# A recommendation tower: Gram products on four strips of the TensorE array in place of two halves, and layer 2 of the last cycle in another order

## The reference

```python
e = jnp.stack([tbl_f[ids[:, f]] for f in range(27)], axis=1)       # (2048, 27, 128)
interactions = jnp.einsum('bnd,bmd->bnm', e, e)                    # a Gram matrix per sample
z = interactions[:, i, j]                                          # i, j: upper triangle, 351 products
h = jnp.concatenate([z, dense_ctx], axis=1)                        # 367 columns
h = jnp.maximum(h @ W_top1 + b_top1, 0.0)                          # 512
h = jnp.maximum(h @ W_top2 + b_top2, 0.0)                          # 256
y = h @ W_top3                                                     # (2048, 1)
```

## Time and profile before

| | |
|---|---|
| median of 3 runs | 348.53 us (348.14 to 349.94) |
| span of the profiled execution | 346.3 us |
| PE busy | 331.1 us, 96% of the span |
| POOL busy | 242.9 us, 70% |
| DVE busy | 219.4 us, 63% |
| ACT busy | 184.7 us, 53% |
| granted TensorE clock, mean | 1.000 |

### The profile page before, as it was taken

One profiled execution on the slowest core, in us unless ns is written; L12 is line 12 of the kernel. 1 busy time (PEld: TensorE's weight loads), 2 busy tenths in 40 slices (PEclk: granted clock), 3 DMA queues, 4 the chain that ended last, 5 costly groups with the idle time before them and its releaser, 6 DMA issues.

```text
span 346.3 us, 8212 instructions
## 1 busy us (share of the span) xinstructions
PE 331.1 (96%) x3478; PEld 282.8 (82%) x3478; DVE 219.4 (63%) x160; ACT 184.7 (53%) x315; POOL 242.9 (70%) x263
## 2 busy tenths in 40 slices
PE   2899999999999999999999999999999999998995
PEld 1667878887898888887898889887888889997894
DVE  5899997599427971499626991399724990360021
ACT  4898975533646354633646355633447346554521
POOL 6777777777777777777777777777777777777200
PEclk9999999999999999999999999999999999999999
DMA  6975795655237772768229772677327552572440
GB/s 169 222 178 168 225 252 142 156 157 135 67 55 157 146 158 55 107 173 178 83 55 157 146 160 55 89 197 177 83 57 134 131 112 57 85 168 72 85 81 8
DMA packets 53981, 44.06 MB, mean 127 GB/s; under 512 B 39810, under 2 KB 43983, under 8 KB 53945
## 3 DMA queue, kind: packets, MB, share of 16 engines
q1 hardware_dynamic: 43993, 26.52, 35.1%
q0 software_dynamic: 8192, 16.79, 21.3%
q10 hardware_dynamic: 1760, 0.22, 0.4%
HBM read 36.43 MB, written 7.09 MB: 126 GB/s over the span
## 4 chain that ended last, share of the span: by engine, by line
PE 86%; DMA 6%; SPq 3%; ACT 2%; issue 1%; DVE 1%; DVEq 0%
PE emb_ps L572 21%; PE emb_ps L574 20%; PE gram_ps L600 16%; PE mlp_ps L617 11%; PE mlp_ps L626 7%; PE emb_ps L583 7%; DMA h<-tbl_rows 3%; DMA products<-gram 1%; DMA gram<-tbl_rows 1%; PE emb_ps L644 1%; SPq L376 1%; DMA z<-products 1%; SPq L369 1%; PE mlp_ps L671 1%; PE mlp_ps L655 1%
## 5 line engine op out<-in xcount | busy, mean ns | idle before, releaser
L543 POOL DMA_INDIRECT rows<-tbl_rows,idx x256 | 242.0, 945 | 78.9 <-issue 74.4
L747 DVE TENSOR_TENSOR onehot<-ids_b,row_id 125x2048 fp32r<-125x2048 int32 x72 | 158.9, 2279 | 33.3 <-PE emb_ps L574 33.3
L572 PE MATMUL emb_ps<-onehot,table_hi 125*128 125x512 f32 (+1 forms) x400 | 147.6, 378 | 5.6 <-DVE table_lo L768 4.0
L574 PE MATMUL emb_ps<-onehot,table_lo 125*128 125x512 f32 (+1 forms) x400 | 143.0, 367 | 0.0
L572 PEld LDWEIGHTS emb_ps<-onehot,table_hi 125*128 125x128 f32 x400 | 76.0, 190 | 21.5 <-DVE table_lo L768 4.8
L574 PEld LDWEIGHTS emb_ps<-onehot,table_lo 125*128 125x128 f32 x400 | 76.1, 190 | 10.7
L600 PEld LDWEIGHTS gram_ps<-emb 128*54 128x54 f32 x2048 | 53.6, 130 | 5.6 <-issue 3.5
L600 PE MATMUL gram_ps<-emb 128*54 128x54 f32 x2048 | 55.8, 214 | 1.7 <-ACT emb L852 0.8
L851 ACT COPY held<-emb_ps 128x256 f32<-128x256 f32 x38 | 14.1, 371 | 75.9 <-PE emb_ps L574 75.8
L784 DVE TENSOR_TENSOR mlp_ps<-mlp_ps,rows 128x256 f32<-128x256 f32 x14 | 6.1, 433 | 76.5 <-PE mlp_ps L626 76.5
L882 ACT COPY gram<-gram_ps 118x432 f32<-118x432 f32 x64 | 33.2, 519 | 39.5 <-PE gram_ps L600 39.2
(11 more groups left out here) (49 smaller groups left out, 102.6 us busy)
## 6 DMA issues: line engine op xcount, KB each, us to landing
ids_b<-ids_onehot SPq DMA_DIRECT2D x33, 256.0 KB, 5.5
products<-gram SPq DMA_DIRECT2D x28, 216.0 KB
gram<-tbl_rows SPq DMA_DIRECT2D x9, 480.0 KB
rows<-tbl_rows,idx POOLq DMA_INDIRECT x256, 2.9
z<-products SPq DMA_DIRECT2D x14, 126.0 KB
h<-tbl_rows SPq DMA_DIRECT2D x2, 480.0 KB
z<-products SPq DMA_DIRECT2D x7, 112.0 KB
w_sb<-w SPq DMA_DIRECT2D x1, 768.0 KB, 5.8
```

Source lines behind the costliest of these rows:

```text
L543: pool.indirect_dma_start(out=rows[:, t, f, :], out_offset=None, in_=gathered_tables[f], in_offset=bass.IndirectOffsetOnAxis(ap=idx[:, p, ...
L572: nc.tensor.matmul(ps[:, 0:width], table_hi[0:ROWS, k, j, :], columns[:, c, :], start=j == 0, stop=False)
L574: last = nc.tensor.matmul(ps[:, 0:width], table_lo[0:ROWS, k, j, :], columns[:, c, :], start=False, stop=j == ROWS_PER - 1)
L747: nc.vector.tensor_tensor(onehot[0:ROWS, seq % ONEHOT_RING, 0:own * width].rearrange("p (j b) -> p j b", b=width), *operands, ALU.is_equal ...
```

## The change

`gram_products` takes one sample at a time. Its 27 columns go to one of four strips of 32 columns of the array and so to PSUM rows 0, 32, 64 or 96 onward. A tile has 128 products in two banks in place of 64 in four, and no mixed blocks. ACT copies a bank in one instruction of 123x432 elements. `gram` takes half the space and shares a tile with the staging buffers of the tables. What is stored and loaded per transfer stays the same size.

In the last cycle, the first tile's part of layer 2 of pair 6 moves from behind the Gram products to both sides of the last turn: two of its four products ahead of it, two behind. ACT's two copies of the dense features move ahead of the copies of the last Gram banks. The third load of the last tile's `z` is issued by ACT instead of SP, and the last tile's layer 1 takes its three steps in the order 0, 2, 1.

```diff
-HALVES, ABREAST = 2, 2
-QUARTERS = HALVES * ABREAST
+STRIPS, STRIP_ROWS = 4, 32
+QUARTERS = STRIPS
 GROUPS = P // QUARTERS
-GRAM_COLS = ABREAST * NF
-HALF_ROWS = P // HALVES
-GRAM_PART = HALF_ROWS + GRAM_COLS
-GROUPS_A_BANK = 8
+GRAM_PART = (STRIPS - 1) * STRIP_ROWS + NF
+GROUPS_A_BANK = 16
...
+LAST_STEPS = ((0, 1, 2), (0, 2, 1))
...
+        def load_step(engine, t, step):
+            first, end = step_places(step)
+            engine.dma_start(z[first:end, step, t * P:(t + 1) * P], tile_entries(t, step)
+                             ).then_inc(last_z_loaded[t][step], 16)
...
-                for step in range(STEPS):
-                    first, end = step_places(step)
-                    sp.dma_start(z[first:end, step, c0:c0 + P], tile_entries(t, step)
-                                 ).then_inc(last_z_loaded[t][step], 16)
+                for step in range(STEPS if t == 0 else STEPS - 1):
+                    load_step(sp, t, step)
...
-                        for half in range(HALVES):
-                            first = group * QUARTERS + half * ABREAST
-                            samples = emb[:, t, first:first + ABREAST, :].rearrange("d s f -> d (s f)")
-                            last = nc.tensor.matmul(
-                                ps[half * HALF_ROWS:half * HALF_ROWS + GRAM_COLS, b * GRAM_COLS:(b + 1) * GRAM_COLS],
-                                samples, samples, start=True, stop=True)
+                        for strip in range(STRIPS):
+                            sample = emb[:, t, group * QUARTERS + strip, :]
+                            row = strip * STRIP_ROWS
+                            last = nc.tensor.matmul(ps[row:row + NF, b * NF:(b + 1) * NF], sample, sample,
+                                                    start=True, stop=True)
...
+            def layer2_part(p, t, k0, k1):
+
+                pe.wait_ge(mlp_taken, p * M1 + M1)
+                for k in range(k0, k1):
+                    last = nc.tensor.matmul(mlp_ps[t][:, 0:HID2], h1[:, k, t * P:(t + 1) * P], w2_sb[:, k, :],
+                                            start=k == 0, stop=k == M1 - 1)
+                if k1 == M1:
+                    last.then_inc(mlp_full, 1)
...
                         layer1(p - 1, m)
-                        turn(p, 1, m)
+                        if p == LAST and m == M1 - 1:
+                            layer2_part(p - 1, 0, 0, M1 // 2)
+                            turn(p, 1, m)
+                            layer2_part(p - 1, 0, M1 // 2, M1)
+                        else:
+                            turn(p, 1, m)
...
-            layer2(LAST - 1)
+            layer2_part(LAST - 1, 1, 0, M1)
...
                 if p < LAST:
                     take_gram(p, 0)
                     place_dense(p)
+                else:
+                    place_dense(LAST)
                 take_gram(p, 1)
...
-            place_dense(LAST)
             for t in range(TILES):
                 for m in range(M1):
                     take_last_layer1(t, m)
+                if t == 0:
+
+                    act.wait_ge(last_products_out[TILES - 1], QUARTERS * 16)
+                    load_step(act, TILES - 1, STEPS - 1)
```

More of the change, by code:

```diff
@@ L201, in build @@
         emb = sb("emb", [P, TILES, P, NF])
-        gram = sb("gram", [P, ABREAST, NF, RUN])
+        stage = sb("stage", [P, STAGES - 1, ROWS_PER * DIM])
+        gram = stage[:, :, :].rearrange("p k c -> p (k c)")[:, 0:NF * RUN].rearrange("p (j g) -> p j g", j=NF)
         z = sb("z", [P, STEPS, PAIR])
@@ L232, in build @@
         part = ROWS_PER * DIM
-        gram_flat = gram[:, :, :, :].rearrange("p s j g -> p (s j g)")
-        stages = [gram_flat[0:ROWS, k * part:(k + 1) * part] for k in range(STAGES - 1)]
+        stages = [stage[0:ROWS, k, :] for k in range(STAGES - 1)]
         stages.append(h1[0:ROWS, :, :].rearrange("p m b -> p (m b)"))
@@ L307, in stored_rows @@
         def stored_rows(q):
-            half, s = divmod(q, ABREAST)
-            row = half * HALF_ROWS + s * NF
+            row = q * STRIP_ROWS
             pad = PAD if q == QUARTERS - 1 else 0
@@ L334, in store_position, with tile_entries @@
             engine.dma_start(last_products[t, to:to + STORE_ROWS, :, q, :],
-                             gram[row:end, q % ABREAST, :, t * GROUPS:(t + 1) * GROUPS]
+                             gram[row:end, :, t * GROUPS:(t + 1) * GROUPS]
                              ).then_inc(last_products_out[t], 16)
+        def tile_entries(t, step):
+            first = step * STEP_FIRSTS[0]
+            offset = ((t * DRAM_ROWS + PAD) * NF + first * (NF + 1) + 1) * P
+            return bass.AP(last_products, offset, [[P, SHIFTS], [(NF + 1) * P, STEP_FIRSTS[step]], [1, P]])
+        def load_step(engine, t, step):
+            first, end = step_places(step)
+            engine.dma_start(z[first:end, step, t * P:(t + 1) * P], tile_entries(t, step)
+                             ).then_inc(last_z_loaded[t][step], 16)
         block = ctx.enter_context(nc.Block())
@@ L375, in store_products @@
                     row, end, to = stored_rows(q)
-                    sp.dma_start(products[p % 2, to:to + STORE_ROWS, :, q, :], gram[row:end, q % ABREAST, :, :]
+                    sp.dma_start(products[p % 2, to:to + STORE_ROWS, :, q, :], gram[row:end, :, :]
                                  ).then_inc(products_out, 16)
@@ L389, in store_tile @@
                     store_position(sp, t, q)
[L391 to L394, removed]
             def load_tile_z(t):
@@ L619, in layer1 @@
                 last.then_inc(mlp_full, 1)
+            def layer2_part(p, t, k0, k1):
[5 more added lines that the diff above has]
+                    last.then_inc(mlp_full, 1)
             def layer2(p):
-                pe.wait_ge(mlp_taken, p * M1 + M1)
                 for t in range(TILES):
[L625 to L628, removed]
+                    layer2_part(p, t, 0, M1)
             def last_layers(t):
@@ L639, in last_layers @@
                     pe.wait_ge(mlp_taken, (LAST + t) * M1)
-                for s in range(STEPS):
+                order = LAST_STEPS[t]
+                for s in order:
                     pe.wait_ge(last_z_loaded[t][s], 16)
@@ L644, in last_layers @@
                         last = nc.tensor.matmul(last1_ps[m][:, 0:P], w1_sb[0:k, s, m * P:(m + 1) * P], z[0:k, s, c0:c1],
-                                                start=s == 0, stop=s == STEPS - 1)
-                        if s == STEPS - 1:
+                                                start=s == order[0], stop=s == order[-1])
+                        if s == order[-1]:
                             last.then_inc(mlp_full, 1)
@@ L882, in take_gram @@
                     nc.scalar.copy(
-                        gram[0:GRAM_PART, :, :, g0:g0 + GROUPS_A_BANK].rearrange("r s j g -> r (s j) g"),
-                        gram_ps[a % GRAM_BANKS][0:GRAM_PART, 0:GROUPS_A_BANK * GRAM_COLS].rearrange(
-                            "r (g c) -> r c g", c=GRAM_COLS)).then_inc(gram_taken, 1)
+                        gram[0:GRAM_PART, :, g0:g0 + GROUPS_A_BANK],
+                        gram_ps[a % GRAM_BANKS][0:GRAM_PART, 0:GROUPS_A_BANK * NF].rearrange(
+                            "r (g c) -> r c g", c=NF)).then_inc(gram_taken, 1)
             def take_layer1(chunk, m):
```

1 line of the change is left out of this document (removed).

## The result

The changed kernel takes 393.5 us (median of four runs, 389.3 to 396.9), the kernel before 348.8 on the same chip: a ratio of 1.124, interval 1.119 to 1.129. The run at 396.9 lies more than 1.5% above the fastest; ratios here leave out such runs (without it the median is 391.8), medians don't. It is some 43 to 45 us slower; the forecast was 346.7. The profiled execution took 389.3 us, its span is 387.5.

The account below looks back on a forecast made before the run. PE and POOL's gathers bound it up to the last turn, then a 22 us chain. 324.3 + 1.37 + 1.9 + 1.78 + 4.83 + 1.4 + 8.85 = 344.45, plus 2.2 gives 346.7 us; range 345.2 to 349.0.

Parts of the forecast that it names:

- I take the low end: Gram products: of 1.86 to 6.7 us a tile, the forecast chose 1.9 in place of 3.37.
- each bound by its columns: Gram products: the halves run side by side at their columns' pace, 0.051 us for 54 columns, 0.029 for 27.
- upper bound of 6.7: Gram products: us a tile if 256 records can't be fed faster than now, 0.0263 us each.
- the rows in pairs of the earlier trace: Program start: matmul records begin in pairs closer than 0.02 us, taken as evidence against a 25 ns limit across strips.
- Fed one by one: Rival, Gram products: instruction stream gives a record per 0.0263 us, 6.7 us a tile, some 400 us; one in ten.
- The two bounds: Before the last turn: PE and POOL's gathers end together, PE within 0.3 us of its earliest possible moment.
- POOL's pace: Gathers: one each 1.25 us whatever PE does, the last starting at 321.6, so the last turn stays at 324.3.
- The tail: Behind the last turn: a chain of PE, ACT and transfers, 22 us long; the span gets 1.8 us shorter.
- the wait for `z`: Ahead of the second tile's last layers: PE ready 3.25 us earlier, `z` only 1.8, so PE waits 1.4 us.
- The 2.2 us above the span: Whole kernel: the median time was taken to stand 2.2 us above the profiled span.
- that case: Last turn: if PE had no wait for the gather there, the moved layer 2 products would delay it by 1.4 us.
- The clock: Rival, last Gram products: at the low clock level they take 1.9 us more, 348.5 us in all; chance 7%.

Follow-up runs that it names:

- more_54: Kernel before, with one more product behind each Gram product, of the same 54 weight columns but two moving columns: 407.3 us, ratio 1.171.
- spread: Changed kernel with all products, each Gram bank placed apart from the next, between layer 1's chunks and layer 2's halves: 369.1 us, ratio 1.062.
- half_products: Changed kernel with every second group of four samples left out of the Gram products, 256 instructions a tile instead of 512: 344.3 us, ratio 0.988.
- tail_only: Kernel before, its Gram products still on two halves of 54 columns, with the changed order of the last cycle: 348.9 us, ratio 1.000.
- shift: Changed kernel with 16 small products of 8 columns added at TensorE's start: 396.6 us (one execution).

## Why the prediction was wrong

**The step that failed** is the choice between the bounds of a tile, "I take the low end". The 1.86 us of columns is nearly right: a bank takes 1.08 us where nothing holds it up, two make 2.16. That is in part luck, since "each bound by its columns" doesn't hold as such: in more_54 a record of two moving columns takes the same 25 ns as one of 54. But busy and idle time of line 600 make 5.4 us a tile (86.5 / 16), most of the way to the upper bound of 6.7. I weighed one question, columns or starts of single records, and the rows in pairs of the earlier trace rows answered that one rightly: 8.4 ns a record, far from one start in 26 ns. What I didn't ask is how many instructions PE gets in a microsecond over a whole tile. A wait that comes once in a block doesn't show in a few stretches of 0.02 us.

A second cost, put at nothing, would have undone the low end by itself: the gathers' pauses. In spread, where most banks are fed in time, a bank of pairs 1 to 7 takes 1.63 us (median) from first to last record, so that two would take some 3.3 us, an estimate, where a tile of before takes 3.37.

**The rival that came true in its numbers** is "Fed one by one": it named the deciding point (over 3.4 us a tile) and some 400 us. Its mechanism is not what the runs show. PE starts records 8.4 ns apart where nothing holds it up, and waits when a block is used up. As evidence for it I gave that the mean of 26 ns is the pace of the stream; it is not, since the strips' records start faster. The sign was elsewhere, in the instruction queue and in the 0.24 us gap of pair 0.

**The feed.** In these traces a packet brings 16.4 KB, 128 weight loads and 128 matmuls lie between gaps, and a block each 3.5 to 4.1 us is about all that PE got, 14 to 16 ns an instruction, where the strips use 4.2. The Trainium skill, "Runtime: NRT & Kernel Launch", section "Instruction fetch mechanics", states the same block (16 KiB, 256 instructions) and that crossing to the next is mostly hidden. The trace agrees with the first and contradicts the second where the strips' products follow each other.

**The two bounds** ahead of the last turn were read rightly, but for POOL's pace, which PE can hold back. Without gathers the kernel before gains nothing (PE alone sets it); with Gram tiles shortened in half_products PE waits for rows, and the last turn stands at 323.96, forecast 324.3 (POOL's last gather at 321.34, forecast 321.6). So even a tile of 1.9 us would have given only the tail.

**The tail** was right in its mechanism. In half_products the wait for `z` costs 1.14 us: from the start of the first tile's layer 2 (line 659) to the second tile's layer 1 it takes 2.86 us (331.59 to 334.45) where it was 1.72; forecast 1.4. Its 344.3 us lie 2.4 below the forecast, and that is in part luck: the last Gram tile (1.3 us instead of 1.9) gives 0.6, the turn 0.3, the wait 0.3, and the last leg, which nobody touched, takes 8.2 us instead of 8.85. The 2.2 us above the span were mis-sized too: each later run has a span of its own, and the time lies 1.8 to 2.0 above it in nearly all. In tail_only, where the tiles keep 3.4 us, the last turn comes 2.4 us later (326.71, 324.32). Of these 0.7 are there from the start (its first tile of pair 1 begins at 93.94, before at 93.29), and 1.7 are the moved products, since PE has no wait there to cover them (the prediction put that case at 1.4); what is gained behind the turn gives that back.

**The clock** was a rival for the tail only, at 1.9 us. It acts elsewhere: the gaps let it fall to 0.50, and the long matmuls behind pay, some 12 us of the 41 together with layer 2's waits. It is a consequence, not the cause: shift's gaps stand where the count puts them, and in pair 0 the first gap and the start of the second lie ahead of the fall.

Left open: what the 1.7 us ahead of a packet and the 1.4 us behind it are spent on, and what in a gather's start stops PE's weight loads. That spread without pair 0's gaps would beat the kernel before is not to be expected: from one cycle's first turn to the next it takes 38.0 us in cycle 1, as before, and 0.7 to 4.8 us longer than before in cycles 2 to 6; its Gram products save 0.5 us there from start to start (6.3 for 6.8), and the work around the four separate banks takes as much more. No run here with all its products beats the kernel before.

## What to carry to other kernels

Splitting a matmul into smaller ones that run side by side saves columns and costs instructions, and the supply of instructions has a rate of its own: here 256 in 3.5 to 4.1 us, with about one block in hand, and an fp32 Gram product is four of them. Before such a change, count the instructions of the stretch, divide by the time that it is to take, and look at the instruction queue's packets and at gaps ended by "issue" in the densest stretch of the kernel as it is. A busy engine with small records also loses the cover that hid other engines' disturbances.

## What the hardware showed that I had not expected

- Four strips of 27 columns ran at 8.4 ns a matmul record (128 in 1.08 us). The Trainium skill, "TensorE: Matmul & The Clock Gate", section "Wait — 56ns, not 53.3ns?", gives about 25 ns as the least from start to start; across strips the trace disagrees.
- A gather's start on GpSimd stops TensorE's weight loads twice for 0.2 to 0.28 us, at full clock; in tiles of 25 ns a record it doesn't show (3.23 and 3.28 us with and without gathers).
- Products of 54 and of 2 weight columns in turn: 0.36 us a pair at full clock, against 0.05 us for a product of 54 columns in two halves (128 records in 3.28 us, two records a product).
